# The routing weights of three expert stages reach the multiply by DMA out of one SBUF partition instead of by a matmul

## The reference, cut to what matters

```python
# layer 0: 8 experts, 128 -> 256 -> 128, gelu, top 2
# layer 1: 64 experts of 64 hidden rows and a shared one of 128, gated
            h = jax.nn.silu(jnp.einsum('th,eih->eti', x, eg_w)) * jnp.einsum('th,eih->eti', x, eu_w)
            routed = jnp.einsum('eti,ehi,te->th', h, ed_w, comb)
# layer 2: 160 experts of 64 hidden rows and a shared one of 64, not gated
        h1 = jax.nn.silu(jnp.einsum('th,eih->eti', x, w_gate))
        h1w = h1 * combine.T[:, :, None]
        routed = jnp.einsum('eti,ehi->th', h1w, w_down)
```

## Time and profile before

| | |
|---|---|
| median of 3 runs | 2404.07 us (2402.37 to 2406.6) |
| the profiled execution | 2406.57 us, its span 2404.8 us |
| granted TensorE clock, mean | 0.873 |
| PE busy | 1962.0 us, 82% |
| DVE busy | 1820.5 us, 76% |
| ACT busy | 1370.3 us, 57% |
| POOL busy | 254.4 us, 11% |
| moved by DMA in the whole span | 37.82 MB |

### The profile page before, as it was taken

The page is one execution under the profiler, slowest core; times in us unless marked ns, Lnnn a source line. Parts: engine busy times, 40 slices in busy tenths (PEclk is TensorE's granted clock), DMA queues, the critical chain, the costliest instruction groups (busy, mean ns, idle before and its releaser), DMA issues. The chain is left out here.

```text
span 2404.8 us, 49561 instructions
## 1 busy us (share of the span) xinstructions
PE 1962.0 (82%) x17365; PEld 1230.6 (51%) x17365; DVE 1820.5 (76%) x4154; ACT 1370.3 (57%) x3474; POOL 254.4 (11%) x321
## 2 busy tenths in 40 slices
PE   6999798576699996674999999996777676774987
PEld 5999644454344443453444444444455354443775
DVE  4444578787699996786888888887777877886776
ACT  5666477234455554644777777775455554553555
POOL 1000111000122221000222222220000000000000
PEclk9999899788699998896999999997878787785785
DMA  2000000100100000000000000000000000000000
GB/s 72 4 4 4 26 18 2 37 1 0 36 23 23 23 16 14 1 1 25 22 20 22 22 22 22 22 15 15 13 0 13 13 0 13 13 0 28 2 1 18
DMA packets 32343, 37.82 MB, mean 16 GB/s; under 512 B 4858, under 2 KB 30074, under 8 KB 31956
## 3 DMA queue, kind: packets, MB, share of 16 engines
q1 hardware_dynamic: 32212, 36.04, 5.1%
HBM read 33.40 MB, written 1.05 MB: 14 GB/s over the span
## 5 line engine op out<-in xcount | busy, mean ns | idle before, releaser
L809 ACT ACTIVATE m_h<-ps 128x512 f32<-128x512 f32 x520 | 310.4, 597 | 281.1 <-PE ps L760 280.9
L829 DVE TENSOR_TENSOR m_hwlo<-m_hw,m_hwhi 128x512 f16<-128x512 f32 x523 | 365.7, 699 | 0.3
L847 DVE TENSOR_TENSOR m_hw<-m_h,ps 128x512 f32<-128x512 f32 x388 | 267.0, 688 | 93.1 <-ACT m_h L809 81.1
L802 ACT ACTIVATE m_hwhi<-m_hw 128x512 f16<-128x512 f32 x523 | 325.4, 622 | 1.5 <-DVE m_hw L847 1.5
L760 PE MATMUL ps<-x_hi,m_whi 128*128 128x512 f16 x652 | 248.6, 381 | 4.6 <-issue 4.4
L760 PE MATMUL ps<-x_lo,m_whi 128*128 128x512 f16 x652 | 248.8, 382 | 0.0
L760 PE MATMUL ps<-x_hi,m_wlo 128*128 128x512 f16 x652 | 248.8, 382 | 0.0
L766 PE MATMUL ps<-m_hwhi,m_whi 128*128 128x512 f16 x529 | 201.6, 381 | 1.7 <-DVE m_hwlo L829 1.7
L766 PE MATMUL ps<-m_hwhi,m_wlo 128*128 128x512 f16 x529 | 200.6, 379 | 0.0
L766 PE MATMUL ps<-m_hwlo,m_whi 128*128 128x512 f16 x529 | 200.3, 379 | 0.0
L786 PE MATMUL ps<-m_combT,m_sel 126*128 126x512 bf16 x520 | 199.3, 383 | 0.0
(11 more groups left out here) (435 smaller groups left out, 4614.5 us busy)
## 6 DMA issues: line engine op xcount, KB each, us to landing
m_stage<-in_m_w SPq DMA_DIRECT2D x97, 128.0 KB, 2.0
m_stage<-in_m_w SPq DMA_DIRECT2D x33, 192.0 KB, 2.3
lj_w<-in_lj_w SPq DMA_DIRECT2D x6, 768.0 KB, 4.3
lq_w<-in_lq_w SPq DMA_DIRECT2D x1, 1536.0 KB, 6.1
m_sel<-in_c_sel_pairs SPq DMA_DIRECT2D x2, 661.5 KB
la_w<-in_la_w SPq DMA_DIRECT2D x1, 1280.0 KB, 5.4
rn_rows<-in_L_attn_rows SPq DMA_DIRECT2D x4, 256.0 KB, 4.3
rn_xs<-rn_xn_hi SPq DMA_DIRECT2D x32, 32.0 KB, 1.9
```

The source lines that it names most:

```text
L802: nc.scalar.activation(hw_hi[:, k % 4, :], hw[:, k % 2, :], ACT.Copy).then_inc(hi_done, 1)
L809: nc.scalar.activation(h[:, k % 2, :], ps[:, 4 + (3 * k % 4 if gated else k % 2), :], func)\
L829: nc.vector.tensor_tensor(hw_lo[:, k % 4, :], hw[:, k % 2, :], hw_hi[:, k % 4, :], ALU.subtract)\
L847: nc.vector.tensor_tensor(hw[:, k % 2, :], src[:, k % 2, :], cb, ALU.mult).then_inc(hw_done, 1)
```

## The change

The matmul with the 0/1 matrix, the matrix itself and the three-part split are gone. The router transposes its float32 matrix as it is into `combT`, where one expert is one partition (layers 1 and 2: even experts on side 0, odd ones on side 1). For each unit SP then issues two DMAs from SBUF to SBUF. Each reads one row of `combT`, 2048 float32 numbers on a single partition, 64 times over and writes it to 64 partitions of the unit's slot of a new tile, `comb`. Line 847 reads that tile. In layers 1 and 2 the shared expert comes first as unit 0, whose weights are a memset of ones.

With this come further moves. The freed PSUM banks let the gate product run ahead (`AHEAD`). `down` trails by four passes. The rest `m_hwlo` of one pass in four (two in layer 1) is taken on POOL. An `activation` on one column stands ahead of the loop. SP's loop is written out unit by unit.

```diff
+        self.cols = [slice(c, EX, sides) for c in range(sides)]
+        self.turns = [(h, c, q) for h in range(2) for c in range(sides) for q in range(2)]
...
-        self.comb, self.parts = sb("comb", [P, NT, self.EX]), sb("parts", [P, NT, NG, 3, GE], BF16)
...
+        self.comb, self.combT = sb("comb", [P, NT, EX]), sb("combT", [P, sides, N])
...
+    def turned(self, n):
+        h, c, q = self.turns[n]
+        at = (2 * h + q) * QW
+        return self.combT[0:self.U, c, at:at + QW], self.S.psum[0:self.U, 4 + n % 4, :]
...
-        n = 0
-        for half in range(2):
-            pe.wait_ge(self.part2, half + 1)
-            for g in range(self.NG):
-                if n >= 4:
-                    pe.wait_ge(self.comb_out[n % 2], (n - 4) // 2 + 1)
-                bank = ps[:, 4 + n % 4, :].bitcast(BF16)
-                for j in range(8):
-                    last = nc.tensor.transpose(bank[0:3 * GE, j * P:(j + 1) * P],
-                                               self.parts[:, 8 * half + j, g].rearrange("p a e -> p (a e)"),
-                                               self.S.identb[:])
-                last.then_inc(self.comb_up, 1)
-                n += 1
+        for n, (h, c, q) in enumerate(self.turns):
+            pe.wait_ge(self.scaled, h + 1)
+            if n >= 4:
+                pe.wait_ge(self.comb_out[n % 2], (n - 4) // 2 + 1)
+            for j in range(4):
+                last = nc.tensor.transpose(ps[0:self.U, 4 + n % 4, j * P:(j + 1) * P],
+                                           self.comb[:, 8 * h + 4 * q + j, self.cols[c]], self.S.ident[:])
+            last.then_inc(self.comb_up, 1)
...
-            act.wait_ge(self.scaled, h + 1)
-            nc.scalar.activation(self.parts[:, halves[h], :, 0, :], self.comb_v(h), ACT.Copy).then_inc(self.part0, 1)
-            act.wait_ge(self.rest1, h + 1)
-            nc.scalar.activation(self.parts[:, halves[h], :, 1, :], self.comb_v(h), ACT.Copy).then_inc(self.part1, 1)
...
+    AHEAD = 2 if gated else 4
+    LAG = 4
+    HB = 2 * UB
+    ON_POOL = (1, 3) if gated else (1,)
+    ON_DVE = tuple(n for n in range(NQ) if n not in ON_POOL)
...
+    comb = sb("comb", [P, UB, N], F32)
...
+    def gate_bank(k):
+        return ps[:, 4 + (2 * (k % 2) if gated else k % 4), :]
+
+    def up_bank(k):
+        return ps[:, 5 + 2 * (k % 2), :]
...
-            sp.dma_start(sel[0:3 * GE], selector).then_inc(sel_got, 16)
-            for u0, bodies, _ in runs:
-                with sp.Fori(0, bodies) as j:
-                    for s in range(UB):
-                        sp.wait_ge(split_done, j * UB + (u0 + s + 1))
-                        sp.dma_start(stage[:, s, :], weights[bass.ds(j * UB + (u0 + s), 1)]
-                                     .rearrange("u p c -> p (u c)")).then_inc(slot_got[s], 16)
+            for u in range(U):
+                s = u % UB
+                sp.wait_ge(split_done, u + 1)
+                sp.dma_start(stage[:, s, :], weights[u]).then_inc(slot_got[s], 16)
+                if halves and u == 0:
+                    continue
+                for part in range(2):
+                    sp.wait_ge(route.comb_out[part], len(route.turns) // 2)
+                sp.wait_ge(hw_done, 4 * u + 4)
+                for half in range(2):
+                    row, side = (u - 1, half) if halves else (u // 2, 0)
+                    sp.dma_start(comb[half * 64:half * 64 + 64, s, :],
+                                 route.combT[row:row + 1, side, :].unsqueeze(1).broadcast_to([1, 64, N]))\
+                        .then_inc(comb_got[s], 16)
...
+            if halves:
+                nc.gpsimd.memset(comb[:, 0, :], 1.0).then_inc(comb_got[0], 32)
+
+            def low(u, n, slot):
+                pool.wait_ge(hi_done, u * 4 + (n + 1))
+                nc.gpsimd.tensor_tensor(hw_lo[:, slot, :], hw[:, n, :], hw_hi[:, slot, :], ALU.subtract)\
+                    .then_inc(lo_pool, 1)
...
+                    for n in ON_POOL:
+                        low(u, n, (4 * s - 4 + n) % HB)
...
-            for u0, bodies, g in runs:
-                with pe.Fori(0, bodies) as j:
-                    for s in range(UB):
-                        pe.wait_ge(split_done, j * UB + (u0 + s + 1 + UB))
-                        for n in range(NQ):
-                            k = 4 * s + n
-                            kk = j * (4 * UB) + (4 * u0 + k)
-                            R = 3 * k if gated else None
-                            hb = ps[:, 4 + (R % 4 if gated else k % 2), :]
-                            cb = ps[:, 4 + ((R + 2) % 4 if gated else 2 + k % 2), :]
-                            pe.wait_ge(hw_done, kk + 1)
-                            product(hb, slice(0, P), s, n).then_inc(gate_done, 1)
-                            if gated:
-                                pe.wait_ge(act_done, kk + 1)
-                                product(ps[:, 4 + (R + 1) % 4, :], slice(P, 2 * P), s, n).then_inc(up_done, 1)
-                                pe.wait_ge(hu_done, kk + 1)
-                            nc.tensor.matmul(cb, sel[0:3 * GE, bass.ds(j * UB + s, 1), :].rearrange("p u m -> p (u m)"),
-                                             combT[0:3 * GE, g, n * QW:(n + 1) * QW], start=True, stop=True)\
-                                .then_inc(comb_done, 1)
-                            pe.wait_ge(lo_done, kk + 1)
-                            down((s if n >= LAG else s - 1) % UB, (n - LAG) % NQ, (k - LAG) % 4)
-            for n in range(NQ - LAG, NQ):
-                pe.wait_ge(lo_done, 4 * U + n)
-                down(UB - 1, n, n)
+            with pe.Fori(0, bodies) as j:
+                for s in range(UB):
+                    pe.wait_ge(split_done, j * UB + (s + 1 + UB))
+                    for n in range(NQ):
+                        k = 4 * s + n
+                        kk = j * (4 * UB) + k
+                        pe.wait_ge(act_done, kk + (5 - AHEAD))
+                        product(gate_bank(k), slice(0, P), s, n).then_inc(gate_done, 1)
+                        if gated:
+                            pe.wait_ge(hu_done, kk + 1)
+                            product(up_bank(k), slice(P, 2 * P), s, n).then_inc(up_done, 1)
+                        wait_low(pe, j * UB + s, n)
+                        down((s - 1) % UB, n, (k - LAG) % HB)
...
+            nc.scalar.activation(warm[:], hw[:, 0, 0:1], func)
...
-                        dve.wait_ge(comb_done, kk + 1)
-                        cb = ps[:, 4 + ((3 * k + 2) % 4 if gated else 2 + k % 2), :]
-                        nc.vector.tensor_tensor(hw[:, k % 2, :], src[:, k % 2, :], cb, ALU.mult).then_inc(hw_done, 1)
-                        dve.wait_ge(hi_done, kk + 1)
-                        low(k - 1)
...
+                        if n == 0:
+                            dve.wait_ge(comb_got[s], j * 32 + 32)
+                        wait_low(dve, j * UB + s, n)
+                        nc.vector.tensor_tensor(hw[:, n, :], src[:, k % 2, :], comb[:, s, n * QW:(n + 1) * QW], ALU.mult)\
+                            .then_inc(hw_done, 1)
+                        m = (n - 2) % 4
+                        if m in ON_DVE:
+                            low(j * UB + (s if n < 2 else s + 1), m, (k - 2) % HB)
...
-    L["c_sel_halves"] = (e == np.arange(16)[None, :, None] // 2 + 0 * m).astype(bf16)
-    L["c_sel_pairs"] = (e == 2 * np.arange(GE // 2)[None, :, None] + m // 64).astype(bf16)
```

More of the change, by code:

```diff
@@ L663, in vector, with experts_phase @@
         weights(1)
[L665 to L681, removed]
-    U, _, COLS = weights.shape
-    NSEL = selector.shape[1]
-    LAG = 3
+        for n in range(0, len(self.turns), 2):
+            out, turned = self.turned(n)
+            dve.wait_ge(self.comb_up, n + 1)
+            nc.vector.tensor_copy(out, turned).then_inc(self.comb_out[0], 1)
+def experts_phase(nc, S, ctx, tag, weights, halves, func, gated, UB, route):
+    U, _, COLS = weights.shape
+    bodies = U // UB
+    assert bodies * UB == U
+    AHEAD = 2 if gated else 4
[3 more added lines that the diff above has]
+    ON_DVE = tuple(n for n in range(NQ) if n not in ON_POOL)
     ps = S.psum
     acc = [ps[:, n, :] for n in range(NQ)]
-    sel_got, zeroed = S.sems.new(f"{tag}_sel_got", f"{tag}_zeroed")
-    gate_done, up_done, comb_done, act_done, hu_done, hw_done, hi_done, lo_done, down_done, split_hi, split_done, \
-        split_start = S.sems.new(*(f"{tag}_{n}" for n in ("gate", "up", "combed", "act", "hu", "hw", "hi", "lo", "down",
-                                                          "split_hi", "split", "split_start")))
+    zeroed = S.sems.new(f"{tag}_zeroed")
+    gate_done, up_done, act_done, hu_done, hw_done, hi_done, lo_dve, lo_pool, down_done, split_hi, split_done, \
+        split_start = \
+        S.sems.new(*(f"{tag}_{n}" for n in ("gate", "up", "act", "hu", "hw", "hi", "lo_dve", "lo_pool", "down",
+                                            "split_hi", "split", "split_start")))
```

(28 more changed lines are left out.)

155 lines of the change are left out of this document (70 added, 85 removed).

## The result

The changed kernel takes **6355.16 us** (median of 4 runs, 6355.04 to 6356.59), against 2403.22 us before (4 runs, 2401.42 to 2406.6): a ratio of 2.6441, with a 95% interval from 2.6396 to 2.6487. The forecast was 6500 us, 145 too much.

What follows compares the result with a forecast made beforehand. PE was taken as the bound before, the new transfers after: 2406.6 less old loops 890.7 and routers 17, plus transfers 4925, tails 30 and weights 43, gives 6497, stated as 6500 us. The range was 3950 to 7100 us.

Steps and rivals of the forecast that it cites:

- What bounds the kernel now: Expert loops before the change: PE alone sets the pace, 6.06 us a unit in m0 and m2, 8.65 in m1.
- The price of a transfer: New DMAs: all bytes leave one source partition at 27.3 GB/s, so 524,288 bytes take 19.24 us.
- The sum: Whole kernel: 2406.6 - 890.7 + 4925 + 30 + 43 - 17 = 6497, stated as 6500 us.
- The tails: Each expert loop's end: some 8 us of work after the last transfer, part of the +30 us.
- The queue: SP's DMA queue: slots let SP issue two units ahead, so DMA engines never pause; landing 90 to 120 us after issue.
- The removed matmul: Expert loops: one matmul fewer in each of 520 passes saves 112.6 us, if PE stays the bound.
- VectorE has seven such instructions a unit: Loops m0 and m2: seven instead of eight, 4.9 us, hidden under PE's 5.2 us a unit.
- the last rival: Expert loops: transfers hidden, POOL's reads slow VectorE by 0.1 us for each of seven instructions; about 2320 us, chance 0.03.
- No bottleneck: New transfers: the source partition doesn't limit, 1.2 to 2.4 us each; 2277 us in all, chance 0.08.
- Gives twice: New transfers: the source partition gives twice the rate, 9.6 us each; about 4030 us in all, chance 0.06.
- gives half: New transfers: the source partition gives 13.7 GB/s, 38.3 us each; some 11,400 us in all, chance 0.06.
- VectorE becomes the bound: Expert loops: transfers hidden, VectorE takes 5.6 us a unit instead of 5.2; about 2320 us, chance 0.03.

Runs made afterwards that it cites:

- e2: Changed kernel with each transfer's rows cut to 4 KB, the rest of `comb` a memset of ones: 3974.59 us.
- e1: Changed kernel with each transfer in layer 2 reading 64 different partitions of `combT` instead of one row 64 times: 3817.58 us.
- e4: Changed kernel with each unit's second transfer reading the neighbouring row in the same group of four partitions: 6359.29 us.
- e3: Changed kernel with each unit's second transfer reading the row four partitions further on: 5531.56 us.
- e6: Changed kernel with `comb` filled with ones once and no transfers into it: 2382.03 us, 0.9919 of the kernel before.
- e8: As e7, with one 1 MB transfer to 128 partitions a unit, its experts on even and odd partitions: 2351.3 us, 0.9793 of the kernel before.
- e9: As e8, but POOL takes no rest in m1 either: 2319.59 us, 0.9654 of the kernel before.
- e7: As e5, with POOL's rest in m0 and m2 given back to VectorE: 2358.05 us, 0.9813 of the kernel before.
- e5: Changed kernel with `combT` copied to device memory once a layer and transfers reading rows there: 2392.11 us, 0.9964 of the kernel before.

## Why the prediction was right, and where it was off

**What bounds the kernel now** held, and m2 of the kernel before at 200.00 of 200 us for PE says so once more.

**The price of a transfer**, 19.24 us, was the forecast. A unit takes 38.7 us including its weights; less the forecast's 0.30 for these, a transfer takes 19.2. No run measures the 0.30 by itself. If 4 KB rows cost half of what 8 KB rows do, e2's 19.4 us leaves 19.3 for a transfer and 0.1 for the weights. e1 shows that the source makes the price, e2 that it goes by bytes. My reason, what one DMA engine does at its own partitions, gave the right rate; the unit that gives it out is wider than I wrote, a group of four partitions (e4 and e3). The Trainium skill ("SBUF — State Buffer", section "Door 1: The DMA port swizzle") puts four neighbouring partitions on one port; e4, e3 and the rows of after agree that this holds for a source. The other four of the eight partitions that the prediction gives a port weren't tried.

**The sum** is 142 us above the profiled 6355.0. In the loops it is 4925 + 30 + 43 = 4998 against 4861.0: 137 too much. The step that was off is "256 x 19.24", taken as one rate throughout. The last unit of each group of four lands early, and that is worth 125 us. A reading that fits e3 and the loops' last units: a unit in flight shares its group with the next unit's transfers, and lands early when these read another group or there are none. No run tests it by itself. Some 12 us remain, 0.1 us a unit, which the weights, perhaps priced 0.2 us too high, can cover. Outside the loops the time fell by 21.9 us, where the routers were put at 17. The tails fit: in m2 the last unit's `m_hw` starts at 5579.82 and the last matmul ends at 5587.63, 7.8 us for 8.

**The queue.** That the DMA engines never pause was right (0.96). Why was not: "two units queued ahead, landing 90 to 120 us" was 45.1, some 2.3 transfers of 19.3. SP is held for 21 us or so in issuing the two transfers of a unit (24.6 at most), so the queue takes fewer transfers than the slots would allow. It costs nothing here, since the queue is never empty.

**The removed matmul** would not have won its 112.6 us, and this is the larger fault. "All this is hidden as long as the new transfers aren't late" is wrong. Loops and all else, each against the profiled execution's own time (us):

| | m0 | m1 | m2 | together | all else |
|---|---|---|---|---|---|
| before | 102.8 | 290.8 | 497.1 | 890.7 | 1515.9 |
| forecast without late transfers | | | | 778.1 | 1498.9 |
| e6, no transfers | 97.7 | 304.7 | 478.9 | 881.3 | 1501.2 |
| e8 | 98.3 | 304.7 | 454.8 | 857.8 | 1495.0 |
| e9, no rests on POOL | 98.7 | 271.6 | 454.0 | 824.3 | 1498.9 |

e6 wins 9.4 us in the loops. The step that failed is "VectorE has seven such instructions a unit: 4.9 us, under 5.2": it takes 5.84, because each rest given to POOL makes VectorE's instructions with two SBUF inputs wait beside it (e7, e8 and e9). I had this under the last rival, at 0.1 us for each of seven and for m0 and m2 alone. Measured it is 0.16 for `m_hw` and 0.30 for `m_hwlo`, and in m1, where I saw no risk, it makes the loop longer than before. The price came from a rest and a split that meet in part; a rest of 128x512 meets more, and the new `m_hw` has two SBUF inputs where the old one had one. By themselves two cost next to nothing: 692 ns in e9's m1, 686 before. The Trainium skill ("SBUF — State Buffer", section "Who interferes with whom") calls the port that these two engines share an exclusive lock, held for the whole instruction. The trace agrees (1.64 us instead of 0.68 in e8), and by that rule the rests should have been priced at POOL's whole duration. That would have been somewhat too much. An estimate from the units: 5.84 - 5.52 x 7/8 = 1.0 us of VectorE for a rest on POOL in m2 (e5, e7), and (9.1 - 8.1 x 10/12) / 2 = 1.2 in m1 (e8, e9), where POOL's own instruction took 1.25 and 1.6 us.

**The rivals.** *No bottleneck*: e5 has such transfers, and takes 2392 us, 0.4% less than before, not the 2277 that I gave this case. *Gives twice* and *gives half*: the 38.7 us unit excludes both. *VectorE becomes the bound*: it does once transfers are no longer late; its price was too small, the time 60 us too low (2382 in e6 against 2320). So had the transfers cost nothing, most of the win would still have been lost.

## What to carry to other kernels

Before a broadcast out of SBUF by DMA, count the source partitions, not only the destinations or the DMA engines: one partition, or four neighbours, gave out 27 GB/s, and the same row from device memory 202 to 214, where VectorE set the pace. Before a piece of VectorE's work goes to GpSimd, look whether VectorE's instructions beside it have two inputs in SBUF; if so, expect VectorE to lose most of GpSimd's duration (here 1.0 to 1.2 us of 1.25 to 1.6), and moving it back can win although VectorE is the bound (34 us from e5 to e7, 32 from e8 to e9). When a matmul is taken off the bounding engine, work out the next engine with durations under the new overlap, not with those of before.

## What was not expected of the hardware

- A source's limit is shared by four neighbouring partitions (6359 us with the neighbour's row, 5532 with the row four further on), and the last unit of a group lands early: 32 to 36.5 us instead of 38.7.
- Reads of two groups, each second transfer, gained 6.4 us of 38.7 a unit, not half. Why no more stays open.
- SP is held for some 21 us, at most 24.6, in issuing two transfers, though their slot has long been free.
- The same 213 and 214 GB/s cost a DMA share of 1.04 when they go to 64 partitions a transfer, and 0.59 when they go to 128.
- VectorE is done sooner with eight instructions a unit (5.5 us) than with seven while POOL does the eighth (5.84 us).
